# When the second layer's row maxima are made: second and third group one stage earlier

## The chip, the cores and the metric

The kernel runs as one program on one core of a Trainium2 chip. The metric is the device time of one execution in microseconds (us), median of several; smaller is better.

## What is computed

Two transformer layers over a sequence of 2048 rows of width 128 in float32, each with attention and a feed-forward part, each part followed by a residual and a layer norm. Layer 0 attends causally, with 8 heads in 2 groups; its feed-forward part works on values quantised in blocks of 16. Layer 1 attends without a mask, with 16 heads of width 8 in 4 groups; its feed-forward part mixes 8 experts.

```python
# layer 0
x = norm(x + attn0(x))               # causal, 2 groups of 4 heads
x = norm(x + fp4_ffn(x))             # silu(xq @ wg.T) * (xq @ wu.T), quantised again, @ wd.T
# layer 1
q = (x @ Wq.T + bq).reshape(b, n, G, hpg, HD)
scores = jnp.einsum('bqghd,bkgd->bghqk', q, k) * scale
attn = jax.nn.softmax(scores, axis=-1)   # 2048 x 2048 for each of 16 heads
x = norm(x + attn @ v @ Wo.T + bo)
x = norm(x + experts(x))
```

## The kernel before

The sequence is cut into 4 chunks of 512 queries (NC = 4), and each chunk's attention runs once for each group: 8 iterations in layer 0, 16 in layer 1. An iteration takes the key tiles (128 keys) one by one and the group's four heads in turn: a score product on TensorE (L812 in layer 0, L816 in layer 1), its exponential on ScalarE (L1032), and later its product with the values (L835), two heads at a time in layer 0 and four in layer 1.

Softmax needs each row's maximum before its exponentials. The kernel finds it ahead, by a second set of score products: one product for 128 queries and 512 keys on TensorE (L731 in layer 0, L726 in layer 1), and one reduction on VectorE (L1282) into MP. In layer 1 a group of one chunk has 64 such maxima: 4 heads, 4 query tiles, 4 key chunks. When all are there, VectorE takes the maximum over key chunks (row_max), TensorE turns it (shift), ScalarE copies it, and a DMA of SyncE puts it as one more row under the queries; only then can the group's iteration begin. The maxima of a group are therefore made while an earlier group's iteration runs, "beside" it. The queries of a group in layer 1 (q1, two products L722 for two pairs of heads) are split in parts by ScalarE (L964, L965) and GpSimd (L1140); the keys (k1, L691) likewise, four groups for each chunk.

In layer 1 the heads lie in two halves of TensorE's 128 rows, so score products and maxima have 64 rows each; in layer 0 they have 96 or 97.

The order of everything is a list of steps (`program`), written by hand and by small rules, and each engine walks this list in order. Scores and side items (maxima, queries, transposes) take the PSUM banks in turn: six in layer 0, seven in layer 1. The parts the change touches:

- `maxima(layer, c, g, it, chunks)` lists a group's maxima, for some key chunks or all; `queries` its queries. Buffer `it` of Q1 holds the queries of group `it`.
- `interleave(behind, many)` puts the steps of `behind`, each with a gap, evenly between the items of `many`.
- `steps0` is layer 0, and at its end the stage between the layers. In its last iteration (chunk 3, group 1) the feed-forward part of chunk 2 (`rest0`: four quantisations of H with their transposes, down, norm1, x2T, k1, v1) runs beside the attention, and with it the first layer-1 maxima. Then comes the stage between: attention's end of chunk 3 (`attended0`: on0, y0, norm0, two quantisations of X, xq, gate, up), then `rest0` of chunk 3, interleaved with more maxima. Until k1 of chunk 3 is there, only key chunks 0 to 2 can be used.
- `steps1(0, True, False)` is the first chunk of layer 1: four iterations of 64 scores, with the maxima of the later groups and of the next chunk's first two groups beside them, cut evenly.

Of the kernel before, what the change touches and what calls it, by code (L numbers as in the profile page):

```python
# [23 lines left out]
NC = T // QC  # L24
# [22 lines left out]
BEGUN = 4  # L47
# [22 lines left out]
def build(nc, A):  # L70
# [3 lines left out]
    with ctx:  # L74
# [146 lines left out]
        def queries(layer, c, g, it):  # L221
            if layer:
                return [("q1", g, c, it, pair) for pair in range(PAIRS)]
            return [("q0", g, c, buffer_of(0, it))]
# [167 lines left out]
        def steps0():  # L392

            part = [(0, c, g, i) for i, (c, g) in enumerate(iters0)]
            work, starts, end = stream(part)

            cuts = [a + int((b - a) * LEAD) for a, b in zip(starts[1:], starts[2:] + [end])] + [end + HG]
            before = between(work, -1, cuts[0])

            opening, second = 2 * QUANT_STAGES, 4 * QUANT_STAGES  # L400
            yield from fold[:4] + before[:2] + fold[4:] + before[2:5] + interleave(ffn_weights[:opening], before[5:])
            carry, outs, behind, begun = [], [], ffn_weights[opening:second], []
            for i, (_, c, g, it) in enumerate(part):
                beside = between(work, cuts[i], cuts[i + 1]) if i < len(part) - 1 else []
                if i == len(part) - 1:

                    begun = [step for _, step in behind[1:QUANT_STAGES]]
                    beside = queries(1, 0, 0, 0) + begun[:1] + maxima(1, 0, 0, 0, range(NC - 2))
                    begun, behind = begun[1:], behind[:1] + behind[QUANT_STAGES:]
                yield from iteration(0, c, g, beside, behind, outs, carry, it, begun)  # L410
                carry, outs = last_products(0, c, g, it), outs0(c, g)
                if g == G0 - 1:
                    behind = attended0(c)
                else:
                    behind = gaps("4", [("on0", 0)]) + (rest0(c - 1) if c else ffn_weights[second:])

            yield from carry + out_copies(outs) + outs
            beside = queries(1, 0, 1, 1) + maxima(1, 0, 0, 0, [NC - 2]) + maxima(1, 0, 1, 1, range(NC - 2))
            yield from interleave(attended0(NC - 1) + rest0(NC - 1), beside)

            work, starts, _ = stream([(1, 0, 0, 0, [NC - 1]), (1, 0, 1, 1, [NC - 2, NC - 1])], False)
            yield from between(work, -1, starts[1] + BEGUN)

        def steps1(c, first, last):

            part = ([(1, c, g, g) for g in range(G1)] + ([] if last else [(1, c + 1, g, g) for g in range(2)]))
            n = len(maxima(*part[0]))
            if first:

                part = [(1, c, 1, 1, [NC - 2, NC - 1])] + part[2:]  # L430
                work, starts, end = stream(part)
                work = [(max(place, BEGUN), s) for place, s in work
                        if s[:3] != ("q1", 1, c) and (place >= BEGUN or s[0] == "q1")]
                work.sort(key=lambda e: e[0])
                till = starts[4] + int(n * LEAD1)
                cuts = [i * till // G1 for i in range(G1 + 1)]
                cuts[0] = BEGUN
            else:
                work, starts, end = stream(part)
                cuts = [n * (g + 1) + int(n * LEAD1) for g in range(G1 + 1)]  # L440
                cuts = [min(cut, end + HG) for cut in cuts]
# [1053 lines left out]
```

## Time and profile before

| | us |
|---|---|
| median of 3 runs | 1398.81 |
| lowest and highest | 1396.12, 1399.25 |
| the profiled execution | 1399.37 |
| its span, first to last instruction | 1397.6 |
| last iteration of layer 0, from its third block of products | 414.03 to 493.87 |
| stage between the layers, to the first score of layer 1 | 493.87 to 597.79 |
| first chunk of layer 1, from its first products | 601.45 to 776.28 |

The page gives busy time by engine and the chain of work that ended last; the windows give both by stretch, with the granted TensorE clock as a share of 2.4 GHz. The timeline gives instructions one by one, runs of equal ones merged.

### The profile page before, as it was taken

To read this page: it belongs to the slowest core of one execution; us is meant where nothing else is said; L and a number is where in the kernel's file an instruction comes from. 1 tells how busy PE (TensorE), PEld (TensorE's weight loads), DVE (VectorE), ACT (ScalarE), POOL (GpSimd) and SP (SyncE) were. 2 spreads that over 40 slices of the span, in tenths; PEclk is the share of its full clock that TensorE was granted. 3 is DMA by queue.
4 is the path that set the end of the run, shared out by engine and by line. 5 is a ranking of instruction groups with operands and counts; after the bars stand their busy time and mean duration, and the time that the engine had idled before them with its cause. 6 is when DMAs were issued, how large, how long until landed. Compare 5 with 4: busy or idle time off the path is not lost.

```text
span 1397.6 us, 19251 instructions
## 1 busy us (share of the span) xinstructions
PE 1273.2 (91%) x6406; PEld 563.6 (40%) x6406; DVE 1051.0 (75%) x2239; ACT 829.9 (59%) x1633; POOL 172.3 (12%) x283
## 2 busy tenths in 40 slices
PE   5689989999999964799999999999999999999896
PEld 3345445445433432433333443344433334334334
DVE  4667886897645569678888888899789888988423
ACT  3334436455555420178888666788666787788760
POOL 5110111103020120100000103000111000000030
PEclk9969989999999976689999999999999999999997
DMA  4010100010000000000000000000000000000000
GB/s 105 18 29 22 25 1 4 21 23 1 1 1 1 1 1 0 0 2 1 1 2 1 1 1 8 1 2 1 1 1 9 1 1 2 1 1 1 1 8 8
DMA packets 10738, 10.85 MB, mean 8 GB/s; under 512 B 2856, under 2 KB 7520, under 8 KB 10640
## 3 DMA queue, kind: packets, MB, share of 16 engines
q1 hardware_dynamic: 9632, 8.84, 2.6%
q0 software_dynamic: 1008, 0.79, 0.3%
q8 instruction: 51, 0.84, 0.3%
q14 instruction: 47, 0.39, 0.1%
HBM read 3.66 MB, written 1.05 MB: 3 GB/s over the span
## 4 chain that ended last, share of the span: by engine, by line
PE 71%; DVE 16%; issue 5%; ACT 5%; POOL 1%; SPq 1%; DMA 1%; DVEq 0%; POOLq 0%; ACTq 0%
PE ps L835 24%; PE ps L816 14%; PE ps L726 10%; DVE MP L1282 8%; PE ps L812 5%; PE ps L731 3%; ACT PR L1032 3%; PE ps L722 2%; PE ps L789 2%; PE ps L755 1%; DVE ps L1279 1%; PE ps L737 1%; PE ps L691 1%; PE ps L766 1%; PE ps L718 1%
## 5 line engine op out<-in xcount | busy, mean ns | idle before, releaser
L1032 ACT ACTIVATE PR<-ps 128x512 f32<-128x512 f32 (+2 forms) x1344 | 697.4, 587 | 370.3 <-PE ps L812 193.5
L1282 DVE TENSOR_REDUCE MP<-ps 128x1 f32<-128x512 f32 x1216 | 764.3, 683 | 139.4 <-PE ps L726 90.5
L835 PE MATMUL ps<-PR,V 128*32 128x512 f32 (+2 forms) x2688 | 433.9, 601 | 3.1 <-ACT OS L921 2.5
L726 PE MATMUL ps<-KO,Q 64*128 64x512 f32 x1024 | 378.9, 460 | 15.3 <-DVE MP L1282 8.2
L816 PE MATMUL ps<-Q,KO 64*128 64x512 f32 x1024 | 339.4, 446 | 8.2 <-DMA Q<-MR 6.0
L816 PEld LDWEIGHTS ps<-Q,KO 64*128 64x128 f32 x1024 | 160.3, 187 | 289.8 <-issue 134.4
L726 PEld LDWEIGHTS ps<-KO,Q 64*128 64x128 f32 x1024 | 170.4, 190 | 95.5 <-DVE MP L1282 33.5
L731 PE MATMUL ps<-KO,QO 96*128 96x512 f32 (+2 forms) x320 | 123.8, 435 | 23.0 <-DVE QO L1263 10.0
L812 PE MATMUL ps<-QO,KO 97*128 97x512 f32 (+3 forms) x320 | 140.2, 453 | 4.1 <-DMA QO<-MR 2.4
L835 PEld LDWEIGHTS ps<-PR,V 128*32 128x32 f32 (+1 forms) x2688 | 74.1, 115 | 129.4 <-issue 62.9
L812 PEld LDWEIGHTS ps<-QO,KO 97*128 97x128 f32 x320 | 61.0, 197 | 130.9 <-issue 80.2
L731 PEld LDWEIGHTS ps<-KO,QO 96*128 96x128 f32 x320 | 64.5, 210 | 43.8 <-DVE QO L1263 11.9
L1111 POOL TENSOR_SCALAR_AFFINE_SELECT PR<-PR 128x128 f32<-128x128 f32 x128 | 39.8, 312 | 332.3 <-ACT PR L1032 331.5
L1279 DVE CUSTOM_DVE_ANT_0 ps<-ps,mask_qk 128x128 f32<-128x128 f32 (+3 forms) x128 | 62.9, 493 | 18.0 <-PE ps L731 17.6
L1140 POOL TENSOR_TENSOR Q<-WHOLE,Q 128x512 fp32r<-128x512 f32 x16 | 20.5, 1282 | 426.2 <-ACT Q L965 426.2
L1103 POOL TENSOR_TENSOR RS<-VE,const 128x4 f32<-128x4 f32 x16 | 16.2, 1014 | 184.6 <-DVE VE L1219 184.6
L789 PE MATMUL ps<-ew,XQT 128*128 128x512 f32 x64 | 37.1, 682 | 0.0
L722 PE MATMUL ps<-XT,WQ 128*128 128x512 f32 x64 | 35.2, 632 | 1.9 <-ACT PR L1032 1.7
L1140 POOL TENSOR_TENSOR Q<-wgu,Q 128x512 fp32r<-128x512 f32 x16 | 20.7, 1296 | 129.1 <-ACT Q L965 129.1
L921 ACT ACTIVATE HQT<-ps 128x256 f32<-128x256 f32 (+3 forms) x37 | 11.2, 350 | 42.0 <-PE ps L761 33.4
L761 PE MATMUL ps<-const,H 128*128 128x128 f32 (+1 forms) x48 | 9.8, 320 | 22.3 <-DVEq L1203 22.3
L1118 POOL TENSOR_TENSOR qa<-qa 128x512 f32<-128x512 f32 (+2 forms) x18 | 14.8, 823 | 115.2 <-DVE XQ L1333 108.2
(201 smaller groups left out, 811.9 us busy)
## 6 DMA issues: line engine op xcount, KB each, us to landing
QO<-Q SPq DMA_DIRECT2D x72, 64.0 KB, 2.0
Q<-MR SPq DMA_DIRECT2D x64, 2.0 KB
result<-V SPq DMA_DIRECT2D x4, 256.0 KB, 2.3
H<-in_L_attn_wq SPq DMA_DIRECT2D x1, 512.0 KB, 3.6
HQT<-in_L_attn_wo SPq DMA_DIRECT2D x1, 512.0 KB, 5.7
ew<-in_L_ffn_expert_w POOLq DMA_DIRECT2D x1, 512.0 KB, 4.2
bq<-in_L_attn_bq POOLq DMA_DIRECT2D x12, 0.1 KB, 3.4
wd<-in_L_ffn_w_down SPq DMA_DIRECT2D x1, 176.0 KB, 4.9
```

The source lines that it names most:

```text
L722: last = nc.tensor.matmul(bank[:, :], WQ13[:, g, pair, :, :], XT[:, c * QC:(c + 1) * QC], start=True, stop=True)
L726: last = nc.tensor.matmul(bank[:, :], Q1[rows, buf, h // 2, q * P:(q + 1) * P], KO1[rows, g, kc * QC:(kc + 1) * QC], start=True, stop=True)
L731: last = nc.tensor.matmul(bank[:, 0:n], QO[0:SHIFT, buf, h, q * P:(q + 1) * P], KO0[0:SHIFT, g, kc * QC:kc * QC + n], start=True, stop=True)
L789: last = nc.tensor.matmul(bank[:, :], X2T[:, q * P:(q + 1) * P], ew[:, 4 * e:4 * e + 4, :], start=True, stop=True)
L812: m = nc.tensor.matmul(dst[:, q0:QC], KO0[:, g, kt * P:(kt + 1) * P], QO[:, buffer_of(0, it), h, q0:QC], start=True, stop=True)
L816: m = nc.tensor.matmul(dst[:, :], KO1[rows, g, kt * P:(kt + 1) * P], Q1[rows, it, h // 2, :], start=True, stop=True)
L835: nc.tensor.matmul(dst, VO[layer][:, kt, g, :], PR[:, u % NP_RING, q0:QC], start=kt == 0, stop=kt == key_tiles(layer, c) - 1).then_inc(pv_ ...
L1032: nc.scalar.activation(PR[:, u % NP_RING, q0:QC], ps[:, bank_of_score[u], q0:QC], ACT.Exp, scale=SCALE[layer]).then_inc(exp_done, 1)
L1111: nc.gpsimd.affine_select(block, block, [[1, P]], ALU.is_ge, nothing, base=0, channel_multiplier=-1).then_inc(clipped, 1)
L1140: nc.gpsimd.tensor_tensor(dst, WHOLE[tails % len(WHOLE)], dst.bitcast(f32), ALU.subtract).then_inc(tailed, 1)
L1279: v.tensor_tensor_reduce(bank[:, 0:w], bank[:, 0:w], mask_qk[:, QC - w:QC], 1.0, LOWEST, ALU.add, ALU.max, MP[:, buf, h, q, kc:kc + 1]).th ...
L1282: v.tensor_reduce(MP[:, buf, h, q, kc:kc + 1], bank[:, 0:w], AX, ALU.max).then_inc(free, 1)
```

## The change

The second group of layer 1 (chunk 0, group 1) gets its queries and its maxima over key chunks 0 and 1 in the last iteration of layer 0, where only the first group's were. In the stage between the layers the third group takes the place that the second had, and the second's maxima over key chunk 2 are made there too. The first chunk of layer 1 loses these steps. By count of maxima: 32 to 64 in the last iteration of layer 0, and 236 to 188 beside the 256 scores of the first chunk of layer 1; the stage between gets 16 more.

```diff
@@ steps0
                     begun = [step for _, step in behind[1:QUANT_STAGES]]
-                    beside = queries(1, 0, 0, 0) + begun[:1] + maxima(1, 0, 0, 0, range(NC - 2))
+                    beside = (queries(1, 0, 0, 0) + begun[:1] + queries(1, 0, 1, 1) + maxima(1, 0, 0, 0, range(NC - 2))
+                              + maxima(1, 0, 1, 1, range(NC - 2)))
                     begun, behind = begun[1:], behind[:1] + behind[QUANT_STAGES:]
...
             yield from carry + out_copies(outs) + outs
-            beside = queries(1, 0, 1, 1) + maxima(1, 0, 0, 0, [NC - 2]) + maxima(1, 0, 1, 1, range(NC - 2))
+            beside = (queries(1, 0, 2, 2) + maxima(1, 0, 0, 0, [NC - 2]) + maxima(1, 0, 1, 1, [NC - 2])
+                      + maxima(1, 0, 2, 2, range(NC - 2)))
             yield from interleave(attended0(NC - 1) + rest0(NC - 1), beside)
 
-            work, starts, _ = stream([(1, 0, 0, 0, [NC - 1]), (1, 0, 1, 1, [NC - 2, NC - 1])], False)
+            work, starts, _ = stream([(1, 0, 0, 0, [NC - 1]), (1, 0, 1, 1, [NC - 1])], False)
             yield from between(work, -1, starts[1] + BEGUN)
@@ steps1
-                part = [(1, c, 1, 1, [NC - 2, NC - 1])] + part[2:]
+                part = [(1, c, 1, 1, [NC - 1]), (1, c, 2, 2, [NC - 2, NC - 1])] + part[3:]
                 work, starts, end = stream(part)
                 work = [(max(place, BEGUN), s) for place, s in work
-                        if s[:3] != ("q1", 1, c) and (place >= BEGUN or s[0] == "q1")]
+                        if s[:3] not in (("q1", 1, c), ("q1", 2, c)) and (place >= BEGUN or s[0] == "q1")]
```

Every line below the first of these stands two lines later in the changed kernel, so L726 becomes L728, and so on.

In the middle of the last iteration of layer 0, TensorE had this order (L835 products, L812 scores, L726 a maximum):

```order
L835 MATMUL ps<-PR,V 64x512 x2
L812 MATMUL ps<-QO,KO 128x512 x2
L726 MATMUL ps<-KO,Q 128x512
L835 MATMUL ps<-PR,V 64x512 x2
L812 MATMUL ps<-QO,KO 128x512 x2
L835 MATMUL ps<-PR,V 64x512 x2
L812 MATMUL ps<-QO,KO 128x512
L726 MATMUL ps<-KO,Q 128x512
L812 MATMUL ps<-QO,KO 128x512
```

In the changed kernel TensorE has this order at the same place (L837 products, L814 scores, L728 a maximum):

```order
L837 MATMUL ps<-PR,V 64x512 x2
L814 MATMUL ps<-QO,KO 128x512
L728 MATMUL ps<-KO,Q 128x512
L814 MATMUL ps<-QO,KO 128x512
L728 MATMUL ps<-KO,Q 128x512
L837 MATMUL ps<-PR,V 64x512 x2
```

A maximum stands behind each score now, where it stood behind every other score or fewer.

In the stage between the layers, VectorE had this order in the first of the four quantisations of H (L1177 to L1198 are its operations, L1282 a maximum):

```order
L1177 TENSOR_REDUCE qs<-H 128x22
L1179 TENSOR_SCALAR qs<-qs 128x22
L1181 RECIPROCAL qr<-qs 128x22
L1282 TENSOR_REDUCE MP<-ps 128x1
L1184 TENSOR_SCALAR qr<-qr 128x22
L1186 TENSOR_TENSOR qa<-H,qr 128x352
L1189 TENSOR_SCALAR qc<-qa 128x352
L1282 TENSOR_REDUCE MP<-ps 128x1
L1191 TENSOR_SCALAR qc<-qc 128x352
L1194 TENSOR_TENSOR qa<-qa,qc 128x352
L1282 TENSOR_REDUCE MP<-ps 128x1
L1196 TENSOR_TENSOR qa<-qa,qc 128x352
```

In the changed kernel VectorE has this order there (L1284 is a maximum):

```order
L1179 TENSOR_REDUCE qs<-H 128x22
L1181 TENSOR_SCALAR qs<-qs 128x22
L1284 TENSOR_REDUCE MP<-ps 128x1
L1183 RECIPROCAL qr<-qs 128x22
L1186 TENSOR_SCALAR qr<-qr 128x22
L1284 TENSOR_REDUCE MP<-ps 128x1
L1188 TENSOR_TENSOR qa<-H,qr 128x352
L1191 TENSOR_SCALAR qc<-qa 128x352
L1284 TENSOR_REDUCE MP<-ps 128x1
L1193 TENSOR_SCALAR qc<-qc 128x352
L1196 TENSOR_TENSOR qa<-qa,qc 128x352
L1284 TENSOR_REDUCE MP<-ps 128x1
```

A maximum comes after every two operations of the quantisation, before after every two or three.

In the first chunk of layer 1, TensorE had this order in most blocks (L835 products, L816 scores, L726 maxima):

```order
L835 MATMUL ps<-PR,V 32x512 x4
L816 MATMUL ps<-Q,KO 128x512
L726 MATMUL ps<-KO,Q 128x512
L816 MATMUL ps<-Q,KO 128x512
L726 MATMUL ps<-KO,Q 128x512
L816 MATMUL ps<-Q,KO 128x512
L726 MATMUL ps<-KO,Q 128x512
L816 MATMUL ps<-Q,KO 128x512
L726 MATMUL ps<-KO,Q 128x512
```

In the changed kernel TensorE has this order in most blocks of that chunk, with L818 the scores:

```order
L837 MATMUL ps<-PR,V 32x512 x4
L818 MATMUL ps<-Q,KO 128x512 x2
L728 MATMUL ps<-KO,Q 128x512
L818 MATMUL ps<-Q,KO 128x512
L728 MATMUL ps<-KO,Q 128x512
L818 MATMUL ps<-Q,KO 128x512
L728 MATMUL ps<-KO,Q 128x512
```

Of four maxima in a block one has gone.

## Rows read from the trace of the kernel before

**Rows 1.** The page: busy time by engine, and the chain that ended last.
```profile
PE 1273.2 (91%) x6406; PEld 563.6 (40%) x6406; DVE 1051.0 (75%) x2239; ACT 829.9 (59%) x1633; POOL 172.3 (12%) x283
...
PE 71%; DVE 16%; issue 5%; ACT 5%; POOL 1%; SPq 1%; DMA 1%; DVEq 0%; POOLq 0%; ACTq 0%
```

**Rows 2.** Windows: stretch, length, busy by engine (instructions), PEclk, DMA share, GB/s.
```profile
414.03:493.87 79.84, 76.75 (x285) 30.77 (x285) 39.05 (x85) 42.80 (x85) 11.59 (x21) 0.96 0.00 1
493.87:597.79 103.92, 59.37 (x191) 31.04 (x190) 75.48 (x177) 15.11 (x31) 11.17 (x10) 0.69 0.00 0
601.45:776.28 174.83, 173.64 (x1044) 67.82 (x1042) 150.39 (x248) 146.14 (x284) 10.34 (x8) 1.00 0.01 1
1275.62:1302.24 26.62, 26.62 (x185) 10.71 (x183) 23.55 (x40) 24.31 (x48) 0.00 (x0) 1.00 0.00 1
```

**Rows 3.** Timeline of TensorE, last iteration of layer 0: start, duration, instruction.
```profile
449.36 1.08 PE L835 MATMUL ps<-PR,V 128*64 128x512 f32 x4
450.37 0.74 PE L812 MATMUL ps<-QO,KO 97*128 97x512 f32 x2
451.04 1.08 PE L835 MATMUL ps<-PR,V 128*64 128x512 f32 x4
...
452.48 0.49 PE L726 MATMUL ps<-KO,Q 64*128 64x512 f32 x1
452.90 0.50 PE L812 MATMUL ps<-QO,KO 97*128 97x512 f32 x1
453.33 0.65 PE L835 MATMUL ps<-PR,V 128*64 128x512 f32 x2
```

**Rows 4.** Timeline of TensorE, same iteration: two maxima of opposite halves.
```profile
477.61 0.50 PE L726 MATMUL ps<-KO,Q 64*128 64x512 f32 x2
478.05 1.08 PE L835 MATMUL ps<-PR,V 128*64 128x512 f32 x4
```

**Rows 5.** Timeline of TensorE, layer 1: where blocks begin, and a query product.
```profile
623.48 1.06 PE L835 MATMUL ps<-PR,V 128*32 128x512 f32 x8
...
626.09 0.64 PE L835 MATMUL ps<-PR,V 128*32 128x512 f32 x4
...
633.89 1.06 PE L835 MATMUL ps<-PR,V 128*32 128x512 f32 x8
...
635.55 1.12 PE L722 MATMUL ps<-XT,WQ 128*128 128x512 f32 x2
...
637.27 1.07 PE L835 MATMUL ps<-PR,V 128*32 128x512 f32 x8
...
1286.77 1.06 PE L835 MATMUL ps<-PR,V 128*32 128x512 f32 x8
...
1288.89 0.64 PE L835 MATMUL ps<-PR,V 128*32 128x512 f32 x4
```

**Rows 6.** Chain in order of time, end of the stage: start, length, what.
```profile
582.93 10.27 DVE MP L1282 x17
```

**Rows 7.** Timeline of TensorE between the gate products.
```profile
524.30 0.79 PE L726 MATMUL ps<-KO,Q 64*128 64x512 f32 x1
...
525.02 1.48 PE L755 MATMUL ps<-WGT,XQT 128*128 128x352 f32 x2
```

**Rows 8.** Timeline, key products of the last iteration of layer 0.
```profile
489.15 0.49 PE L726 MATMUL ps<-KO,Q 64*128 64x512 f32 x1 [0.77 <-POOL KO L1140]
...
489.80 1.27 POOL L1140 TENSOR_TENSOR KO<-wgu,KO 128x512 fp32r<-128x512 f32 x1 [0.45 <-ACT KO L965]
```

**Rows 9.** Timeline, key products of the stage between the layers.
```profile
577.45 0.77 PE L726 MATMUL ps<-KO,Q 64*128 64x512 f32 x1 [2.79 <-POOL KO L1140]
```

**Rows 10.** Timeline, start of that stage: first query's ScalarE work, ONT, y0.
```profile
499.10 0.69 ACT L964 ACTIVATE WHOLE<-ps,bq 128x512 f32<-128x512 f32 x1 [2.04 <-PE ps L722]
...
500.35 0.60 ACT L921 ACTIVATE ONT<-ps 128x512 f32<-128x512 f32 x1
...
501.19 2.05 PE L744 MATMUL ps<-WVO,ONT 128*128 128x128 f32 x16
```

## The prediction

> **What bounds the kernel now.** I read the page first, then the stretches, then single instructions. The page puts TensorE at 91% busy and on 71% of the chain, VectorE at 75% and 16% [rows 1]. An average over stages decides nothing here, since the change only moves 48 maxima (a maximum is one TensorE product, L726, and one VectorE reduction, L1282) between three stages. The table of stretches shows the three apart [rows 2]. In the last iteration of layer 0, less its first blocks (414.03 to 493.87), TensorE is busy 76.75 of 79.84 us and VectorE 39.05: TensorE bounds it. In the stage between the layers (493.87 to 597.79) VectorE is busy 75.48 of 103.92 us and TensorE 59.37, at a mean granted clock of 0.69, so for part of the time at its lower level of 1.2 GHz. In the first query chunk of layer 1 (601.45 to 776.28) TensorE stands at 173.64 of 174.83 us, VectorE at 150.39 and ScalarE at 146.14: all three near their limit, and what a block costs is read from blocks of either kind.
>
> I call a block what lies from one run of products (L835) to the next. In layer 0 a block has two scores (S) and some maxima (M). P S S is 1.68 us (449.36 to 451.04), P S M S is 2.29 us (451.04 to 453.33) [rows 3]. So a lone maximum costs 0.43 us (452.48 to the next score at 452.90), and it costs 0.20 more where it parts two scores. Two maxima of opposite halves stand as x2 at 477.61 and the products follow at 478.05: 0.44 us for both [rows 4]. In layer 1 a block has four scores; maxima and scores of opposite halves overlap. With four maxima it takes 2.61 us (623.48 to 626.09), with three 2.12 us (1286.77 to 1288.89) [rows 5].
>
> **The change, part A: the first chunk of layer 1 gets 48 maxima fewer.** In the order of the program its 64 blocks held 236 maxima: 43 blocks with four or five, 21 with two or three. Now they hold 188: 9 with four, 55 with two or three. The bare blocks before sum to 43 x 2.61 + 21 x 2.12 = 156.7 us; the stretch took 174.83 [rows 2], so 18.1 us go to nine query products, four output copies and four shifts. Nothing prices the last eight apart; I put them at 0.4 each (my choice), which leaves 1.65 for a query product. Its own block took 3.38 (633.89 to 637.27), 0.8 above 2.61 [rows 5]; the rest falls on the blocks behind. Seven queries are left: extras 18.1 - 3.3 = 14.8 us. The new bare blocks are like twelve of the last chunk, ten with three maxima and two with four, that took 26.62 us, 2.22 each, with ScalarE at 24.31 of it [rows 2]: 64 x 2.22 = 142.0; from the single prices, 55 x 2.12 + 9 x 2.61 = 140.1. I take 141.5 + 14.8 = 156.3. **A = -18.5 us.** It can't be much more: ScalarE, with 24.31 of 26.62, is then the limit, and a maximum less buys nothing below three in a block. Ends: -13 (were a block 2.30) and -24 (were a query 1.1 and the blocks as at their single prices).
>
> **Part B: the last iteration of layer 0 gets 32 maxima and two query products.** By the order, TensorE's maxima stood in 30 places there (28 alone, 2 pairs); now they stand in 52 (39 alone, 11 pairs, one run of three, counted as two). 22 places x 0.43 = 9.5 us. Blocks whose two scores are parted go from 17 to 29: 12 x 0.20 = 2.4 us. Two query products (L722, two passes, 1.12 us with the end of the second) [rows 5], of which I take 0.85 as their place in the queue: 1.7 us. Then the tail: the product that makes keys of group 1 (L691) stood four instructions ahead of a maximum that needs group 0's keys, which waited 0.77 us for GpSimd's subtraction [rows 8]. Now a maximum of group 1 stands directly behind group 1's key product. Behind that product come two ScalarE operations and the 1.27 us of GpSimd, which ended at 491.07 where the old wait ended at 489.15 [rows 8]: 2.0 us. **B = +15.6 us.** VectorE hides its 32 x 0.68 = 22 us: 39 + 22 = 61 of some 95 us. If that cover fails, see the third rival. Ends: +11 (places and queries alone) and +24 (every maximum alone and parting scores, 32 x 0.63, and the rest).
>
> What speaks against the move is a rule of the Trainium skill, TensorEngine Tiling (Array Packing), Key Properties: changing the tiling mode, not just the tile, drains the engine. The rows agree: a score behind a score adds 0.24 us (x2 takes 0.74, one 0.50) [rows 3], a lone 64-row product 0.43. Were no drain paid, 22 x 0.24 would stand for 9.5 and nothing for the parted scores: B = 8, the first rival.
>
> **Part C: the stage between the layers gets 16 more (48 become 64, before the 20 at its end, which stay).** VectorE walks two quantisations of X and four of H there, whose operations form one chain with maxima put between. A maximum on a full VectorE takes 0.60 us (17 in 10.27) [rows 6]. By VectorE's order, 3 more lie before the transposes of XQ and 6 more within the four quantisations of H: 9 x 0.60 = 5.4. One more lies between the gate products, where TensorE is the path at the lower clock: 0.72 (524.30 to 525.02) [rows 7]. One more lies between the second residual's statistics and its norm: 0.6. Two more lie about the key products of the last chunk, and the maximum that waits there now needs group 2's keys, not group 1's; before, TensorE waited 2.79 us at that place [rows 9]. The third subtraction on GpSimd adds 1.27, but one key product moves ahead of the wait and fills it: I take 0.8. At the stage's start both query products now stand ahead of the transposes of ON, so ScalarE makes its copy (ONT, 500.35 to 500.95) behind the second query's two operations, which take 1.25 us (499.10 to 500.35 for the first query's) [rows 10]; the product of y0 began at 501.19, 0.24 after the copy's end: 1.0, and two more maxima hide in it. One hides under the down product. Sum 5.4 + 0.7 + 0.6 + 0.8 + 1.0. **C = +8.5 us.** Ends: +1 (the 28 us in which VectorE idles take them all) and +13.
>
> The group 2 queries go to the tile that also held the moved halves of layer 0's queries; the last of these moves is long past, and no DMA or queue of SyncE is added or passed: 0. GpSimd's subtractions are as many as before.
>
> **Sum.** -18.5 + 15.6 + 8.5 = +5.6 us. The profiled execution took 1399.37 us for a span of 1397.6; the median of the three runs is 1398.81, 0.56 lower. Against the median: 1404.4 us.
>
> **Rivals.**
> 1. *The added maxima cost TensorE only their columns in layer 0.* If the scores beside them waited anyway, a maximum would cost 0.24, not 0.43, and part none: B = 22 x 0.24 + 1.7 + 1 = 8, sum -2, and with A at -24 it is -7.5: 1391 to 1397, faster. Against it: TensorE has 3 us idle in 80, and 0.43 repeats in the blocks. It decides from B below 7.2, or below 12.7 with A at -24.
> 2. *The clock.* More products in the middle stage keep TensorE at 2.4 GHz for more of it. A mean of 0.69 is 1.2 GHz for 62% of the stage [rows 2]; of the path in it I estimate some 16 us to be TensorE's at that level (XQ, gates, down, keys); half of these saved makes C about +0.5, sum -2.4: 1396.4, and faster with any of the other ends. Against it: the added ones are 16 x 0.4 to 0.7 us in 104 us, with VectorE still ahead of them. The rule that activity raises the clock and idleness lowers it stands in the Trainium skill, TensorE: Matmul & The Clock Gate, What's actually happening; the clock of 0.69 beside 59 of 104 us busy agrees.
> 3. *Banks in layer 0.* Scores and maxima take six banks in turn. With four maxima in a block a score waits for a VectorE that in the last third also has the residual, statistics and norm. At 0.25 us for each of 28 blocks: +7, sum +12.6: 1411, slower still.
> 4. *VectorE's idle time takes part C.* With C at +1 to +4 the sum is -1.9 to +1.1: 1397 to 1400, no change. For it: 28 us idle. Against it: the idle pieces lie where it waits for TensorE's down and key products, and only two of the 16 land there.
>
> **How the numbers follow.** Forecast 0.55, its own range 1398 to 1408; rival 1 0.10, rival 2 0.10, rival 3 0.15, rival 4 0.10. What a measurement here can tell from no change is about 0.2%, 2.8 us: below 1396.0 faster, above 1401.6 slower. Of the forecast 0.15 falls within and 0.40 above. Rival 1 is faster, rival 2 half faster (0.05) and half within; rival 3 slower; rival 4 within (0.08) or faster (0.02). Faster 0.17, same 0.28, slower 0.55. The range 1396 to 1411 leaves out most of rival 1, half of 2 and the far end of 3.
>
> **What the profile after would show.** A: blocks of 2.1 to 2.2 us in the first chunk of layer 1, its stretch near 156 us, ScalarE above 0.9 busy. B: the iteration from the same point near 95 us, P S M S M at 2.72 us, TensorE without gaps. C: from the last products to layer 1's first score near 113 us, VectorE busy some 85. I am wrong if B comes out below 10 or above 20, if a layer-1 block with three maxima stays above 2.3, or if the clock in the middle stage rises.

## The result

The changed kernel takes 1408.47 us (median of 4 runs, 1407.30 to 1409.19) against 1397.62 for the kernel before (4 runs, 1396.12 to 1399.25): ratio 1.0082, 95% interval 1.0066 to 1.0098. It is slower by 10.9 us where I had forecast 5.6. The profiled execution took 1408.93 us for a span of 1407.2, so the spans of the two profiles differ by 9.6; all stretches below are read from these two.

The page after: busy time by engine, and the chain that ended last, to be laid beside [rows 1].

```profile
PE 1282.8 (91%) x6406; PEld 568.4 (40%) x6406; DVE 1050.5 (75%) x2239; ACT 830.2 (59%) x1633; POOL 171.8 (12%) x283
...
PE 72%; DVE 16%; issue 5%; ACT 4%; POOL 1%; DMA 1%; SPq 1%; DVEq 0%; POOLq 0%; ACTq 0%
```

No engine has another share of busy time, the chain moves by one per cent (TensorE 72 for 71), and TensorE's 9.6 us more are of the same instructions, so the page tells nothing of the place. The windows do. First the three stretches of after that answer to those of [rows 2] (the stage now up to layer 1's first products, 511.88 to 631.29, which before was 493.87 to 601.45), then the rest of the program.

```profile
413.24:511.88 98.64, 93.53 (x321) 37.78 (x320) 57.48 (x117) 46.93 (x89) 15.40 (x25) 0.93 0.00 1
511.88:631.29 119.41, 76.02 (x221) 39.82 (x220) 87.29 (x198) 17.93 (x36) 9.89 (x9) 0.63 0.00 0
631.29:783.69 152.40, 151.90 (x993) 59.99 (x991) 122.57 (x200) 142.25 (x280) 7.73 (x6) 1.00 0.00 1
...
783.69:1407.20 623.51, 595.03 (x3356) 242.12 (x3355) 487.44 (x910) 435.77 (x839) 68.83 (x76) 0.97 0.01 3
```

The kernel before, in the stage to the first products and in the rest:

```profile
493.87:601.45 107.58, 63.03 (x204) 33.82 (x203) 78.24 (x182) 17.94 (x37) 11.17 (x10) 0.68 0.00 0
...
776.28:1397.60 621.32, 592.61 (x3356) 242.20 (x3355) 487.64 (x910) 435.55 (x839) 68.96 (x76) 0.97 0.01 3
```

| us | before | after | difference | forecast |
|---|---|---|---|---|
| iteration (B) | 79.84 | 98.64 | +18.8 | +15.6 |
| stage between (C) | 107.58 | 119.41 | +11.8 | +8.5 |
| first chunk of layer 1 (A) | 174.83 | 152.40 | -22.4 | -18.5 |
| the rest | 621.32 | 623.51 | +2.2 | 0 |

With the 0.8 by which the iteration starts earlier, that is the 9.6. The rest has the same instructions (x3356). Its 2.2 is the balance of a few blocks where low stretches of the clock fell otherwise: two took 2.8 and 1.6 us more, others less.

In the middle of the iteration, TensorE after:

```profile
450.48 1.08 PE L837 MATMUL ps<-PR,V 128*64 128x512 f32 x4
451.49 0.49 PE L814 MATMUL ps<-QO,KO 97*128 97x512 f32 x1
451.91 0.50 PE L728 MATMUL ps<-KO,Q 64*128 64x512 f32 x1
452.34 0.50 PE L814 MATMUL ps<-QO,KO 97*128 97x512 f32 x1
452.77 0.50 PE L728 MATMUL ps<-KO,Q 64*128 64x512 f32 x1
453.20 1.08 PE L837 MATMUL ps<-PR,V 128*64 128x512 f32 x4
```

From products to products this is 2.72 us, as forecast from [rows 3]: 1.01 for the products, then 0.43 four times. At the iteration's end stands what I had sized too small:

```profile
499.71 1.07 PE L693 MATMUL ps<-XT,WK 128*128 128x512 f32 x2
503.57 0.49 PE L728 MATMUL ps<-KO,Q 64*128 64x512 f32 x1 [2.79 <-POOL KO L1142]
503.99 0.65 PE L837 MATMUL ps<-PR,V 128*64 128x256 f32 x4
...
504.74 1.71 PE L693 MATMUL ps<-XT,WK 128*128 128x512 f32 x2
506.38 0.79 PE L728 MATMUL ps<-KO,Q 64*128 64x512 f32 x1
...
507.37 2.02 PE L693 MATMUL ps<-XT,WK 128*128 128x512 f32 x2
```

The maximum waits 2.79 us for GpSimd's part of the keys, where [rows 8] had 0.77. That is the 2.0 us of the prediction. But soon behind it the key product takes 1.71 us instead of 1.07 and the maximum 0.79 instead of 0.49: the idle time is followed by the lower clock, and what is left of the iteration runs at it. At the end of the stage the same wait stands again, as in [rows 9], but TensorE passes it 8.95 us after the first key product (598.32 to 607.27), which before were 6.13 (571.32 to 577.45):

```profile
598.32 2.07 PE L693 MATMUL ps<-XT,WK 128*128 128x512 f32 x2
...
601.05 3.44 PE L693 MATMUL ps<-XT,WK 128*128 128x512 f32 x4
607.27 0.67 PE L728 MATMUL ps<-KO,Q 64*128 64x512 f32 x1 [2.78 <-POOL KO L1142]
607.88 2.07 PE L693 MATMUL ps<-XT,WK 128*128 128x512 f32 x2
```

One key product and one maximum moved ahead of this wait, and the wait is as long as before.

In the first chunk of layer 1 blocks begin at these times. One with three maxima takes 2.11 us (641.91 to 644.02), as the single price said (2.12), and the next, with a query product and two maxima, 3.37:

```profile
641.91 1.06 PE L837 MATMUL ps<-PR,V 128*32 128x512 f32 x8
...
644.02 1.06 PE L837 MATMUL ps<-PR,V 128*32 128x512 f32 x8
...
647.39 1.07 PE L837 MATMUL ps<-PR,V 128*32 128x512 f32 x8
```

So a query product adds 1.26 us to its block. It did so before too: the block that the prediction read (633.89 to 637.27, 3.38 us) held three maxima beside its query product, these two instructions, and not four:

```profile
634.89 0.49 PE L726 MATMUL ps<-KO,Q 64*128 64x512 f32 x1
...
636.61 0.73 PE L726 MATMUL ps<-KO,Q 64*128 64x512 f32 x2
```

That is 1.26 above the 2.12 of a block with three, not 0.8 above the 2.61 of one with four.

### The profile page after: what moved, and what is told of

It is laid out like the page before. It is cut to its first block, busy times and chain, and to the rows that moved or that the text cites. A ratio compares the mean times of both kernels' runs of the same rounds, so it can differ in the third digit from the quotient of the medians.

```text
span 1407.2 us, 19254 instructions
## 1 busy us (share of the span) xinstructions
PE 1282.8 (91%) x6406; PEld 568.4 (40%) x6406; DVE 1050.5 (75%) x2239; ACT 830.2 (59%) x1633; POOL 171.8 (12%) x283
## 4 chain that ended last, share of the span: by engine, by line
PE 72%; DVE 16%; issue 5%; ACT 4%; POOL 1%; DMA 1%; SPq 1%; DVEq 0%; POOLq 0%; ACTq 0%
PE ps L837 24%; PE ps L818 14%; PE ps L728 10%; DVE MP L1284 8%; PE ps L814 6%; PE ps L733 3%; PE ps L724 2%; ACT PR L1034 2%; PE ps L791 2%; PE ps L757 1%; PE ps L693 1%; PE ps L739 1%; DVE ps L1281 1%; PE ps L768 1%; DVE ST L1212 1%
## 5 line engine op out<-in xcount | busy, mean ns | idle before, releaser
L1284 DVE TENSOR_REDUCE MP<-ps 128x1 f32<-128x512 f32 x1216 | 766.9, 683 | 153.8 <-PE ps L728 107.4
L837 PE MATMUL ps<-PR,V 128*32 128x512 f32 (+2 forms) x2688 | 435.1, 604 | 2.5 <-ACT OS L923 2.5
L728 PE MATMUL ps<-KO,Q 64*128 64x512 f32 x1024 | 380.9, 467 | 17.1 <-DVE MP L1284 9.6
L818 PE MATMUL ps<-Q,KO 64*128 64x512 f32 x1024 | 332.8, 448 | 8.2 <-DMA Q<-MR 6.1
L818 PEld LDWEIGHTS ps<-Q,KO 64*128 64x128 f32 x1024 | 155.6, 187 | 288.0 <-ACT PR L1034 132.4
L728 PEld LDWEIGHTS ps<-KO,Q 64*128 64x128 f32 x1024 | 170.4, 192 | 99.3 <-DVE MP L1284 37.5
L814 PE MATMUL ps<-QO,KO 97*128 97x512 f32 (+3 forms) x320 | 143.1, 456 | 4.1 <-DMA QO<-MR 2.4
L837 PEld LDWEIGHTS ps<-PR,V 128*32 128x32 f32 (+1 forms) x2688 | 74.5, 116 | 132.4 <-issue 62.4
L814 PEld LDWEIGHTS ps<-QO,KO 97*128 97x128 f32 x320 | 62.1, 197 | 133.9 <-issue 81.4
```

The costliest lines, as they stand in the source:

```text
L728: last = nc.tensor.matmul(bank[:, :], Q1[rows, buf, h // 2, q * P:(q + 1) * P], KO1[rows, g, kc * QC:(kc + 1) * QC], start=True, stop=True)
L814: m = nc.tensor.matmul(dst[:, q0:QC], KO0[:, g, kt * P:(kt + 1) * P], QO[:, buffer_of(0, it), h, q0:QC], start=True, stop=True)
L818: m = nc.tensor.matmul(dst[:, :], KO1[rows, g, kt * P:(kt + 1) * P], Q1[rows, it, h // 2, :], start=True, stop=True)
L837: nc.tensor.matmul(dst, VO[layer][:, kt, g, :], PR[:, u % NP_RING, q0:QC], start=kt == 0, stop=kt == key_tiles(layer, c) - 1).then_inc(pv_ ...
L1284: v.tensor_reduce(MP[:, buf, h, q, kc:kc + 1], bank[:, 0:w], AX, ALU.max).then_inc(free, 1)
```

## The experiments

Theory: the parts add, each maximum at the price of its stage, and what is missing in my sum is the key waits and the low clock behind them. Rivals: the tail's clock sets the stage behind it; VectorE's idle time could take the stage's maxima; activity could raise the clock. The windows of the experiments stand together at the end of this section. Each ratio is to the kernel before, timed on the same chip as the experiment. Its median was 1398.72 beside the parts alone and the key waits, 1395.67 beside the placing, the doubled products and the changed kernel with both edits, 1397.06 beside the other kernels with both edits and 1396.68 where one of these was timed again. Differences between kernels of different groups are therefore good to 2 or 3 us only.

**One part alone.** Part B alone keeps the stage's 48 maxima:

```diff
-            beside = (queries(1, 0, 2, 2) + ... + maxima(1, 0, 2, 2, range(NC - 2)))
+            beside = (queries(1, 0, 2, 2) + ... + maxima(1, 0, 2, 2, [0]))
...
-                part = [(1, c, 1, 1, [NC - 1]), (1, c, 2, 2, [NC - 2, NC - 1])] + part[3:]
+                part = [(1, c, 1, 1, [NC - 1]), (1, c, 2, 2, [1, 2, 3])] + part[3:]
```

> Only part B is done: the last iteration of layer 0 as in the changed kernel (64 maxima, four query products), the stage between the layers with its 48 maxima as before, and the first chunk of layer 1 with 32 maxima fewer than before (204 for 236). My theory, that the three parts add and that each maximum has its own price in its stage: B +18.8 us as the changed kernel showed, the stage 107.6 as before, the first chunk 32/48 of -22.4 = -15; sum +4, so 1401 to 1403, and the wait of 2.79 us at the key products of the last iteration is there again. Rival (the clock that falls in the tail of part B sets the stage behind it): the stage is 110 to 112 us although its maxima are those of before, sum +7 to +8. Rival (a maximum buys more in the first chunk where a block falls from four to three than from three to two): the first chunk gives back under -12, sum +7 as well, but with the stage at 107.6.

Part C alone keeps the iteration of before. Its 16 maxima more are of the second group, key chunk 2 (the two later lists that had this chunk lose it, not shown), so unlike the changed kernel it has no maxima of a third group in the stage, and it has no query product more than the kernel before, whose two stand there already (the expectation says otherwise):

```diff
-            beside = queries(1, 0, 1, 1) + maxima(1, 0, 0, 0, [NC - 2]) + maxima(1, 0, 1, 1, range(NC - 2))
+            beside = queries(1, 0, 1, 1) + maxima(1, 0, 0, 0, [NC - 2]) + maxima(1, 0, 1, 1, range(NC - 1))
```

> Only part C is done: the last iteration of layer 0 as before, the stage between the layers with two more query products and 64 maxima (before 48), the first chunk of layer 1 with 16 maxima fewer. My theory: the iteration 79.8 as before; the stage longer by the priced +8.5 (116 us from the last products of layer 0 to the first of layer 1), since the 3.3 us that the changed kernel showed beyond it came from the clock that part B's tail had left low; the first chunk 16/48 of -22.4 = -7.5 or less; sum about +1, 1398 to 1401. Rival (16 maxima and a subtraction in the stage cost more than I priced): the stage is 119.4 as in the changed kernel, sum +4. Rival (VectorE's idle time takes them): stage 108 to 111, sum -4 to -7, faster.

B alone: 1401.32 us, ratio 1.001 (0.9991 to 1.0029); C alone: 1399.73, ratio 1.0007 (0.9993 to 1.0021). By the windows B alone costs 18.8 in the iteration and gives back 16.1 in the first chunk, for 32 maxima and two query products; its stage took 105.84, 1.7 less than before. The rival of the tail's clock had the stage at 110 to 112 and falls as a whole, but not in its mechanism: up to the product of y0 the steps are those of before, and they took 8.85 us (511.66 to 520.51) where they took 7.32 (493.87 to 501.19), with products at the lower clock. (The kernel before with exact waits, below, took 8.52 there behind a tail at full clock, so the tail is not all of it.) What made the stage shorter is in its waits. At its key products, where the kernel before waited 2.79 us [rows 9], part B alone has this:

```profile
590.72 3.38 PE L693 MATMUL ps<-XT,WK 128*128 128x512 f32 x4
594.03 0.50 PE L728 MATMUL ps<-KO,Q 64*128 64x512 f32 x1
594.46 1.98 PE L693 MATMUL ps<-XT,WK 128*128 128x512 f32 x4
```

The maximum at 594.03 is one of the third group, whose key product of this chunk comes only behind it in the program, so it waits for nothing.

C alone costs 9.4 in its stretch up to the first products of layer 1, but 3.1 of that is a query product, which in this order comes ahead of the first products and not behind them:

```profile
603.62 2.07 PE L722 MATMUL ps<-XT,WQ 128*128 128x512 f32 x2
```

Up to layer 1's first score it is 6.3 (110.25 us, 491.37 to 601.62, against 103.92), and the layer's first chunk from that score on gives back 2.0, since this query product at the lower clock costs 1.8 more than one of 1.26. The 6.3 lie above the rival's 0 to 3 and below my 8.5, of which 0.8 was for the third group. In medians each half by itself is a wash.

But 6.3 - 1.7 is not 11.8: together they cost 7.2 us more in the stage than apart. The timelines, cut at the same products in all four kernels, show where. Up to y0 they simply add (C alone 1.1, B alone 1.5, both 2.8), and in VectorE's chain up to the first key product it is C's 6.2 in both. Nearly all of the surplus, 6.9, is at the key products: from the first of them to the maxima behind the value products, C alone takes 0.4 less than before (10.91 us), B alone 3.3 less, both 3.2 more. C alone has the changed kernel's order there, but its maximum waits for two subtractions and not for three:

```profile
583.75 0.49 PE L726 MATMUL ps<-KO,Q 64*128 64x512 f32 x1 [1.43 <-ACT KO L965]
584.17 1.12 PE L691 MATMUL ps<-XT,WK 128*128 128x512 f32 x2
```

It passes the wait 7.60 us after the first key product (576.15 to 583.75), the changed kernel after 8.95: the third subtraction is 1.35. And from there to the maxima behind the value products it takes 2.91 us (to 586.66), the changed kernel 5.17 (607.27 to 612.44), for the same products: the wait of 2.78 us is followed by the lower clock, the wait of 1.43 is not.

**The key waits.** Maxima wait by a name; that of a key product had the group alone, so that a maximum on chunk 0 waited for the group's latest key product, whatever its chunk. Now each waits for its own chunk's:

```diff
-            if kind in ("k0", "k1", "on0", "out0", "hqT", "wqT"):
+            if kind == "k1":
+                return item
+            if kind in ("k0", "on0", "out0", "hqT", "wqT"):
...
-                return [("q0", b), ("k0", g)] if layer == 0 else [("q1", b, h // 2), ("k1", g)]
+                return [("q0", b), ("k0", g)] if layer == 0 else [("q1", b, h // 2), ("k1", g, kc)]
```

> The changed kernel, with one rule of the order's waits made exact: a maximum waits for the key product of its own key chunk, not for the last key product of its group. The computation is the same. My theory: both waits of 2.79 us (in the last iteration of layer 0 and in the stage) go, and with the first the fall of the clock behind it: the iteration 98.6 to about 93, the stage 119.4 to about 116; sum -5 to -9, 1400 to 1404. Rival (what ends there is VectorE or the banks anyway, and the wait only moves one step on): -1 or less. Rival (only the idle time goes, the clock falls as before): -5.6 at most, with blocks of the tail at the lower level still.

> The kernel before, with the same exact rule. My theory: its waits of 0.77 us in the last iteration and 2.79 us in the stage go: -2 to -4, so 1394 to 1396. Rival (the stage is bound by VectorE's maxima behind the keys, which can't start sooner for all but three of them): within 1 us of the kernel before.

On the changed kernel: 1390.60 us, ratio 0.9945 (0.9924 to 0.9967). On the kernel before: 1391.58, ratio 0.9943 (0.9925 to 0.9962). Both are beyond what I expected (5 to 9 and 2 to 4 us off, against 17.9 and 7.1 by the medians). By the windows it is 5.9 in the iteration and 7.6 in the stage of the changed kernel, 0.7 and 3.6 in that of before. For the changed kernel the two profiles differ by 15.9 in all; the 2.3 beyond the stretches lie ahead of the iteration (413.24 against 410.96), in steps that the edit doesn't touch. The tail of the changed kernel's iteration with exact waits:

```profile
498.88 0.65 PE L839 MATMUL ps<-PR,V 128*64 128x256 f32 x4
...
499.62 1.07 PE L695 MATMUL ps<-XT,WK 128*128 128x512 f32 x2
...
503.66 0.65 PE L839 MATMUL ps<-PR,V 128*64 128x256 f32 x4
```

The wait has gone and the same key product takes 1.07 again: of the 5.9 us, 2.8 are the wait and 3.1 the lower clock behind it (the last block is 4.78 us long, 7.89 in the changed kernel, from 503.99 to 511.88). The rival that only the idle time goes is out for the iteration. With exact waits the change costs the iteration 13.6 us (92.70 against 79.10), which is just the forecast's places, parting and queries (9.5 + 2.4 + 1.7), and the stage 7.8 (111.83 against 104.00), with the old waits 18.8 and 11.8.

**Where the maxima stand in a block.** In the last iteration of layer 0, side steps wait for the block's second score:

```diff
+                    first, after = slot - HG, slot - HG + 1
+                    if layer == 0 and c == NC - 1 and g == G0 - 1:
+                        first, after = (first, first) if slot % 2 == 0 else (first - 1, after)
-                    yield from late[n * (slot - HG) // m:n * (slot - HG + 1) // m]
+                    yield from late[n * first // m:n * after // m]
```

> The changed kernel, with the side steps of the last iteration of layer 0 put behind both scores of a block instead of behind each: P S S M M where it had P S M S M, so that no maximum parts two scores and the two maxima, of opposite halves, stand side by side. My theory (a lone maximum 0.43 us, 0.20 for parting, a pair of opposite halves 0.44 for both): such a block falls from 2.72 to 2.12 us, some 22 blocks, so the iteration from 95 to about 82 us, 12 to 14 us less than the changed kernel. Rival (the maxima cost their columns whatever their place): 0. Rival (with two scores and two maxima in a row the exponentials come too late for the next products, or six banks don't do): blocks near 2.4, -6.

> The kernel before, with the same placing. Its blocks of P S M S (2.29 us) become P S S M (1.68 + 0.43 = 2.11), and the few of P S M S M become P S S M M. My theory: 17 places x 0.20 = -3.4 us, and 0.4 more for each of three new pairs: about -4. Rival (parting costs nothing): 0.

The changed kernel's blocks with this placing:

```profile
448.86 1.08 PE L840 MATMUL ps<-PR,V 128*64 128x512 f32 x4
...
450.53 0.73 PE L731 MATMUL ps<-KO,Q 64*128 64x512 f32 x3
451.19 1.08 PE L840 MATMUL ps<-PR,V 128*64 128x512 f32 x4
452.20 0.73 PE L817 MATMUL ps<-QO,KO 97*128 97x512 f32 x2
452.87 0.50 PE L731 MATMUL ps<-KO,Q 64*128 64x512 f32 x2
453.30 1.08 PE L840 MATMUL ps<-PR,V 128*64 128x512 f32 x4
```

With two maxima 2.11 us (451.19 to 453.30), with three 2.33. The same work took 2.72 with a maximum behind each score. The iteration is 7.9 us shorter (98.64 to 90.70; the expectation's 95 and 82 count from the block behind), not 13: such blocks with scores parted by one maximum are 14 before the quantisations end, at 0.61 each 8.5, and I had counted 22; behind them keys, norm and their waits hold the path. The wait of 2.79 us and the low clock behind it stayed. The time is 1394.42 us, ratio 0.998 (0.9963 to 0.9997), 14 below the changed kernel, of which the stages explain 6.6. On the kernel before, the iteration is 3.4 shorter (1392.40 us, ratio 0.9969, 0.9952 to 0.9986). That this is 17 x 0.20 is chance: its six plain blocks of P S M S fell by 0.19 to 0.20 each, three that got a new pair by 0.61 to 0.63, and those whose scores transposes or key products had parted by nothing. Both rivals of no effect fall, and with blocks of 2.11 so does that of late exponentials, though the whole gain is nearer its 6 than my 12 to 14: the 0.43 and 0.20 are costs of the place.

**The clock of the stage.** Each maximum product of the stage is issued twice, the second time into a bank that nobody reads; so TensorE has 83 products more there (I had counted 80; the trace has x303 for x221 and misses one) and no other engine anything.

```diff
                     side_item(step, n, k)
+                    if step == ("out0", 1, NC - 1, G0 - 1) or kind == "shift":
+                        stage[0] = kind == "out0"
+                    if kind == "max" and stage[0]:
+                        rows = band_of(step[2])
+                        nc.tensor.matmul(ps[:, OUT_BANKS[step[2] % 2], :], ..., start=True, stop=True)
```

> The changed kernel, with each of the 80 maximum products of the stage between the layers issued a second time, into a bank that nobody reads there; VectorE's work is the same, and the output too. It tells the clock from VectorE in that stage. My second rival (activity of TensorE brings the clock back): the mean granted clock of the stage rises from 0.63 to 0.8 or more, and the stage of 119.4 gets 5 to 10 us shorter, although TensorE has more to do. Against it (the time of the stage is VectorE's chain, and TensorE's second products lie in its idle time): stage 118 to 121 with the clock as it was. If TensorE is the path for much of it and the clock stays low: 124 or more.

1409.72 us, ratio 1.0089 (1.0064 to 1.0113); the stage 122.73, 3.3 longer, at a mean granted clock of 0.65 for 0.63, though TensorE is busy 86.62 us there, 10.6 more. My second rival falls for this amount of activity. The 122.73 also lies above the 118 to 121 of the case against it: the 10.6 us more of TensorE cost 3.3, about the gates and the key products, where it is the path, and the other two thirds lie beside VectorE's work.

**Both edits.** The changed kernel with both edits, and beside it the kernel before and two others with both. These expectations count the iteration from its fourth block of products, 3.6 us later than the windows, so their 72, 77 and 82 us are 75.6, 80.7 and 85.7 in the table.

> Both on the changed kernel: side steps behind both scores of a block, and each maximum waits for the key product of its own chunk alone. If the two are independent, -13 for the first and -14 to -18 for the second: 1376 to 1382 us. If the placing takes its gain from the same tail in which the wait stood: 1382 to 1388.

> Both edits on the kernel before: side steps behind both scores of a block in the last iteration of layer 0, exact waits for the key products. It tells what the change itself is worth once a second maximum in a block costs nothing there and the key waits are gone. From the runs so far the iteration should be 72.8 less the 0.77 of its wait = 72, the stage 104, the first chunk of layer 1 175: 1386 to 1389 us. Against it stands the changed kernel with both (77.1, 111.1, 153.3), which should then be the faster by 175 + 104 + 72 - 341.5 = 9 us in those stages. Rival (the change is a loss or nothing whatever stands around it): the two within 2 us.

> Part B alone with both edits. If the 16 maxima of part C cost VectorE 7.5 us in the stage (111.1 against 104 without them) and save TensorE 22.4 - 16.1 = 6.3 us in the first chunk, then taking part C away is worth 0.5 to 1.5 us: iteration 77, stage 104, first chunk 159.5; 1381 to 1384. Rival (a maximum saved in layer 1 is worth more than one in the stage costs): 1386 or more.

> The changed kernel with both edits, and 16 of the stage's maxima (third group, first key chunk) with the third group's two query products moved on into the last iteration of layer 0: 80 maxima there, 48 in the stage, 188 left in the first chunk. My theory: the third maximum of a block costs TensorE 0.22 us (2.33 for P S S M M M against 2.11), so the iteration rises by 16 x 0.22 + 1.7 = 5 to 82 us, and the stage falls by 7 to 9 to about 103; 1379 to 1382. Rival (VectorE, now with 39 + 48 x 0.68 = 72 us in the iteration, becomes its bound in the last third, where it also has the norm): the iteration 86 or more, 1384 or more.

The last of these moves the third group's queries and first key chunk on into the iteration:

```diff
-                              + maxima(1, 0, 1, 1, range(NC - 2)))
+                              + maxima(1, 0, 1, 1, range(NC - 2)) + queries(1, 0, 2, 2) + maxima(1, 0, 2, 2, [0]))
...
+            beside = maxima(1, 0, 0, 0, [NC - 2]) + maxima(1, 0, 1, 1, [NC - 2]) + maxima(1, 0, 2, 2, [1])
```

> The same kernel as in the run of the kernel before with both edits, timed once more, since its six times reached from 1377 to 1396 us and its profiled execution (1395.9) was the slowest of them. If the change is worth something once both edits stand around it, as the sum of the three stages says (351.5 us against 341.5), this median is 1384 or more, with a ratio above 0.9905, against 0.987 and 0.989 of the two changed kernels with both edits. If the change is worth nothing there, the ratio is 0.989 or less.

| kernel, with both edits | us | ratio to before | 95% interval | iteration, stage, first chunk |
|---|---|---|---|---|
| before | 1384.66 | 0.9907 | 0.9875 to 0.9940 | 75.57, 103.89, 175.70 |
| before, timed again | 1389.11 | 0.9953 | 0.9934 to 0.9972 | 75.54, 103.89, 175.74 |
| changed | 1383.59 | 0.9892 | 0.9863 to 0.9922 | 80.77, 111.12, 153.27 |
| part B alone | 1380.59 | 0.9872 | 0.9858 to 0.9887 | 83.73, 102.10, 159.41 |
| 16 maxima more into the iteration | 1386.03 | 0.9920 | 0.9908 to 0.9932 | 94.42, 105.72, 152.82 |

The three stretches of the changed kernel sum to 345.2 us, those of the kernel before with the same edits to 355.2. But 3.0 of these 10 us are no gain of the change. In all fourteen profiles TensorE idles 2.31 or 2.32 us ahead of the iteration's fourth block; in thirteen the lower clock follows, and in that of the changed kernel with both edits it does not. First the changed kernel, then the changed kernel with both edits:

```profile
416.87 1.98 PE L837 MATMUL ps<-PR,V 128*64 128x512 f32 x4 [2.31 <-ACT OS L923]
...
410.87 1.08 PE L842 MATMUL ps<-PR,V 128*64 128x512 f32 x4 [2.31 <-ACT OS L928]
```

Part B alone with both edits has the same iteration step for step and takes 83.73 us, 2.96 more, all of it in the two blocks behind this wait. Set equal, the change with its faults mended pays 7 us in the stretches, where I had expected 9. Part B alone is 2.9 us ahead of the changed kernel in stage and first chunk (261.5 against 264.4), and has the lowest median, 1.3% below the kernel before: the stage is no place for the 16 maxima, the iteration is one for 32.

Whole times say less. Those of the kernel before with both edits reached from 1376.68 to 1395.86, and its first ratio (0.9907) can't be told from the changed kernel's (0.9892). Twelve more runs gave 0.9953 (0.9934 to 0.9972), above the intervals of both changed kernels; but only the kernel before was timed again, and its own two ratios lie further apart than its first lies from the changed kernel's. The changed kernel's 1383.59 is 25 us below the 1408.47 without the edits, less than the 17.9 and 14 of the two edits alone, and lies in the second of the ranges that I had given, though in the stretches their gains add (iteration 5.9 + 7.9, measured 14.9 without the 3.0).

The 16 maxima moved on into the iteration don't pay. The iteration was 8.7 us over my 82 (94.42 against 85.7), some 3 of it the clock at its start, which the kernel that I reckoned from had not lost; another 3.4 stand at a maximum that waits for its group's query product, with the lower clock behind it:

```profile
488.46 0.50 PE L732 MATMUL ps<-KO,Q 64*128 64x512 f32 x1 [1.94 <-POOL Q L1146]
...
490.30 1.98 PE L841 MATMUL ps<-PR,V 128*64 128x512 f32 x4
```

Its block (482.55 to 490.30) took 7.8 us, and the products behind it already run at the lower clock. The iteration and the 1386.03 us are in my rival's ranges. VectorE, which it named, was busy 63.92 of 94.42 us there, so it is no bound of the whole; in the last blocks it has a part, for the last five maxima take TensorE 2.29 us (503.52) and the five before them 0.96. The remaining 2 us I did not take apart.

The windows of the experiments, columns as in [rows 2]. Part B alone, all three stretches:

```profile
413.01:511.66 98.65, 93.54 (x321) 37.79 (x321) 57.46 (x117) 46.98 (x89) 15.41 (x25) 0.93 0.00 1
511.66:617.50 105.84, 64.55 (x204) 35.83 (x203) 78.20 (x182) 17.83 (x36) 9.94 (x9) 0.63 0.00 0
617.50:776.27 158.77, 158.35 (x1008) 62.73 (x1006) 132.18 (x216) 143.04 (x280) 7.73 (x6) 1.00 0.01 1
```

Part C alone, stage and first chunk:

```profile
491.37:608.35 116.98, 74.03 (x222) 37.05 (x221) 87.07 (x197) 19.53 (x39) 12.38 (x11) 0.67 0.00 0
608.35:778.16 169.81, 169.42 (x1026) 65.52 (x1026) 141.81 (x232) 143.81 (x282) 9.08 (x8) 0.99 0.00 1
```

Exact waits on the changed kernel, iteration and stage:

```profile
410.96:503.66 92.70, 90.38 (x321) 36.46 (x320) 57.46 (x117) 46.86 (x89) 14.35 (x24) 0.96 0.00 1
503.66:615.49 111.83, 70.54 (x220) 36.98 (x219) 87.36 (x198) 17.93 (x37) 11.00 (x10) 0.66 0.00 1
```

Exact waits on the kernel before, iteration and stage:

```profile
411.50:490.60 79.10, 76.78 (x285) 30.78 (x285) 39.03 (x85) 42.80 (x85) 11.57 (x21) 0.96 0.00 1
490.60:594.60 104.00, 62.46 (x205) 34.65 (x204) 78.22 (x182) 17.90 (x37) 11.24 (x10) 0.66 0.00 0
```

The new placing on the changed kernel, iteration:

```profile
411.37:502.07 90.70, 84.92 (x321) 34.22 (x320) 56.76 (x117) 44.68 (x89) 15.47 (x25) 0.91 0.00 1
```

The new placing on the kernel before, iteration:

```profile
411.54:487.96 76.42, 73.39 (x286) 29.09 (x285) 38.75 (x85) 41.68 (x85) 11.74 (x22) 0.96 0.00 1
```

Maximum products twice in the stage of the changed kernel:

```profile
510.23:632.96 122.73, 86.62 (x303) 50.46 (x302) 87.33 (x198) 17.94 (x36) 9.87 (x9) 0.65 0.00 0
```

## Why the prediction was right, and where its terms were off

The direction held, and the measured 1408.5 lies in the range of 1396 to 1411, though just above the forecast's own 1398 to 1408. The size came out at twice the forecast. In the stretches both losses were sized too small, by 3.2 and 3.3 us, and the gain too small by 3.9, so two errors partly cancelled; that the sum stayed in the range is in part luck. The rest of the miss lies outside the stretches: 1.4 in the rest of the program and ahead of the iteration, and 1.3 because the profiled execution of the kernel before took longer than any of its four runs.

A block here is what the prediction calls one, and the bare blocks are those without their query products, copies and shifts.

- **A, -18.5, was -22.4.** Two terms failed. The bare blocks came at the single prices (three maxima 2.11 to 2.19 us, four 2.60), so they sum to 140.1 and not to the 141.5 that I took. And the query product at 1.65 us: 152.4 - 140.1 less 3.2 for copies and shifts leaves 1.3 for each of seven, and a query's block shows 1.26. I had this in hand and misread it, setting a block of three maxima and a query against one of four maxima. My "a maximum less buys nothing below three" was wrong too: the blocks with two maxima and nothing else took 1.89 to 1.95 us.
- **B, +15.6, was +18.8.** The places at 0.43 and the parting at 0.20 held: the block of 2.72 us came exactly, and with exact waits the change costs the 13.6 that these and the queries sum to. The wait of 2.0 held too. The miss is the lower clock behind this wait, 3.1 us by the kernel with exact waits; 3.2 were missing. My condition "TensorE without gaps" failed here.
- **C, +8.5, was +11.8.** VectorE's terms held: 6.2 us more between y0 and the first key product, for 5.4 + 0.7 + 0.6. The step that failed is "one key product moves ahead of the wait and fills it: I take 0.8". Against part C alone the third subtraction cost 1.35 us and the lower clock behind its wait 2.3, and part C alone saves 1.0 from the key products to layer 1's first score. The start of the stage, 1.0 in my sum, took 2.8: 1.2 more than with part B alone, as forecast, and 1.5 that part B alone shows too, from products at the lower clock. Why the clock is low there stays open.
- **The rivals.** The first (a maximum costs its columns) falls with the blocks, the second (activity brings the clock back) with the doubled products, the third (banks in the iteration) with 2.71 to 2.73 us in 14 blocks without a wait, the fourth (VectorE's idle time) with part C alone at +6.3.
- **The rule on the tiling mode** (the Trainium skill, TensorEngine Tiling (Array Packing), Key Properties) would say that P S M S M switches twice more than P S S M M. The rows give 0.61 us for these two switches and the lost pairing together, and the experiment shows that the cost goes when the steps are regrouped; how much of it is the draining that the page names, no run here tells apart.

Open stays why the whole time moved more than the three stretches in several kernels (17.9 us by the medians for the exact waits, 13.5 in the stretches). Part of it is there before any edit acts: in the fourteen profiles the iteration begins between 407.24 and 414.03 us, behind the same steps. In the profiles it is low stretches of the clock at other blocks; what places them was not tried.

## What to carry to other kernels

Count what parts two products of one kind, not only what is added: a second maximum in a block of layer 0 cost 0.62 us or 0.01, depending on whether it stood between the scores or beside its fellow. When work moves to an earlier stage, look at what its waits are tied to; a wait named by group and not by piece cost 3.5 us of the three stretches where few steps stood at it, and 13.5 when the new steps did. Price a wait on TensorE with the lower clock that may follow it, here 2.3 to 3.1 us behind waits of 2.3 to 2.8. Compare stretches cut at the same instructions, and look whether an instruction crossed the cut; a whole time of this kernel moves by some us of itself.

## What the runs showed of the hardware

A gap of 2.79 us was followed by 1.2 GHz for the rest of the iteration (a key product's pair 1.07, then 1.71 and 2.02 us); a gap of 0.77 in the kernel before was not, nor one of 1.43 with part C alone (1.12 for the pair). Behind the same gap of 2.31 or 2.32 us the clock was low in thirteen profiles and full in one (1.98 and 1.08 us for four products). In the stage, TensorE busy 86.62 of 122.73 us had a mean clock of 0.65, and busy 76.02 of 119.41 one of 0.63. In layer 0 a pair of 64-row products of opposite halves costs what one costs (2.11 and 2.10 us for the block), and a third adds 0.22.
